# Couplings and inverse products of the two head halves alternate on eight 32x32 tiles of the TensorE array; query turns as transposes

## The chip, the cores and the metric

One core of one Trainium2 chip runs the whole program. The metric is the device time of one execution in microseconds. The kernel before takes 2709.87 us, the median of 3 runs (2707.37 to 2710.03).

## What is computed

Input is x of shape 2 x 4096 x 512 (two sequences, b = 0 and 1). A routing layer, a recurrent attention layer and the routing layer again are applied, each on the layer-normed x and added to it. The attention layer is the part that the change touches, for each of 16 heads of width 32:

```
q, k, v = xWq, xWk, xWv per head; q and k scaled to length 1
alpha = sigmoid(x @ Wa + ba); beta = sigmoid(x @ Wb + bb)
for each row t:                       # state: 32 x 32 for each b and head
    pred  = state . k_t
    state = alpha_t * state + beta_t * (v_t - pred) k_t
    y_t   = state . q_t
out = (rmsnorm(y) * silu(x @ Wg)) @ Wo
```

## The kernel before, in words

The rows of a sequence go through in 32 tiles of 128, each cut into 4 chunks of 32 rows. In a chunk the recurrence is solved in closed form: the couplings of its keys with its keys and queries (a 32 x 64 product for each head and chunk), the inverse of a unit triangular 32 x 32 matrix, the inverse applied to values and keys, and products that carry the result into the output and the state. All of these have 32 x 32 stationary operands, so each uses one of the 16 tiles of the TensorE array: its row quarter is that of the operands' 32 partitions, its column quarter that of the output's 32 partitions. A 32-bit product is two MATMUL records in the trace, each with its weight load; a transpose by TensorE is one.

**Work on TensorE.** `gram` (L913, its matmuls L926) makes the couplings: for each head, chunk c of the keys times chunk c of keys and queries, written to partitions of chunk c. So it uses the four tiles (c, c) of the diagonal. It comes in 4 pieces of 4 heads for each b; heads 0 to 7 lie in one PSUM bank, 8 to 15 in another. `apply_uw` (L931, matmuls L945) applies the inverse, again on the four diagonal tiles. `qe_T` (L950, L961) turns the decayed queries by a plain matmul with the identity, 8 blocks of 128 x 128 in a step. `apply_gy` (L964, matmuls L976 and L983) makes the two sorts of products that need no state; in each of its four rounds r, heads 0 to 7 use tiles (c, c+r) and heads 8 to 15 tiles (c, c+r+2), eight tiles in turn. `chain` (L987, L996) brings the state in, chunk by chunk, on four diagonal tiles; between two of them VectorE turns the new state (`state`, L2556). `dec` (L905) sums decays with a triangular mask. `project` (L845, L847), `proj_g` (L891), `out_proj` (L1011), `hidden` (L1028), `logits` (L1040), `cum` (L899), `ffn` (L836), `slots` (L1048) and the transposes `first_xT`, `last_xT` (L690) are full-size products.

**The way round VectorE and memory.** After `gram`, VectorE multiplies the couplings by masks (`coupling` L2516 into `nn`, `reading` L2524 into `pk`). SyncE's queue stores `nn` of both b in memory and loads them as `blk` with one matrix on each partition (L517, L523). VectorE inverts all 128 matrices there, 30 pairs of small operations (`invert` L2530; L2540, L2542), with other work in between. SyncE stores the result (L531) and loads it back as `E` (L537), and `apply_uw` uses it one step later. GpSimd makes the masks and scaled keys (`beta_mask` L2036, `decay_mask` L2042, `key_written` L2052) and the powers for the norms (`key_power`, `query_power`, L1977).

**Order.** Every engine and SyncE's queue run an order written out by hand: `step_pe` (L1433), `step_dve`, `step_act`, `step_pool`, `step_sp`, one step for each tile, with tiles p, q, r, s of different age in one step, p the newest; `first_...` and `last_...` hold the ends. `free(...)` and `since(...)` are the waits that keep buffers and PSUM banks from being overwritten. `step_pe` before runs, with b behind the tile's letter: uw r0 (4 pieces), va q1, gy r0 round 0, va and k q1, then gy r0 rounds 1 to 3 with gram q0 pieces 0 and 1 between them, q projection q1 (4), chain r0.0, dec q0, chain r0.1, gram q0.2, chain r0.2, dec q1, gram q0.3, logits s1, chain r0.3, gram q1 (4), uw r1 piece 0, cum, out r0.0, uw r1 (3), y_norm r0 and out r0 with query turns r1 between them, gy r1 rounds 0 and 1, slots, gate, gy r1 rounds 2 and 3, gate, ffn, then chain r1.0 to r1.3 with gate products, a transpose of alpha and last_xT between them, and the rest of the full-size work, in it logits r0 and the query turns q0. The last before the next step's uw is the query turn q0.

Of the kernel before, what the change touches and what calls it, by code (L numbers as in the profile page):

```python
# [27 lines left out]
P = 128  # L28
# [7 lines left out]
def build(nc, x, Wq, Wk, Wv, Wa, ba, Wb, bb, Wg, Wo, g_norm, slot_init, slot_scale, w1, b1, w2, b2,  # L36
          wih, whh, bih, bhh, wv, bv, wo, bo, tau, out):
    ctx = ExitStack()
    with ctx:
# [33 lines left out]
        after = sb("after", P)  # L73
        chunk = sb("chunk", P)
# [48 lines left out]
        glx = sb("glx", NC * B * H)  # L123
        vk3 = [vk[b][:, :].rearrange("p (m h e) -> p m h e", m=3, h=H) for b in range(B)]
# [74 lines left out]
        hold_in, e_in = sem2("hold_in"), sem2("e_in")  # L199
        sl_ps, sums1, aT_ps, aT = sem("sl_ps"), sem("sums1"), sem("aT_ps"), sem("aT")  # L200
# [8 lines left out]
        ffn_at = [banks(1, 1), banks(2, 1)]  # L209
        xT_at = [banks(1, 1), banks(7, 1)]  # L210
        k_at = [banks(6, 1), banks(0, 1)]
        q_at = [banks(4, 1), banks(4, 1)]
        va_at = [banks(1, 1), banks(5, 1)]
        vb_at = [banks(5, 1), banks(4, 1)]
        g_at = [banks(0, 1), banks(7, 1)]
        dec_at = [banks(5, 1), banks(0, 1)]
        ones_at = [banks(1, 1)[:, 0:1], banks(6, 1)[:, 0:1]]
        wo_at = [banks(2, 1), banks(0, 1)]
        rxT_at = [banks(1, 1), banks(0, 1)]
        h_at = [banks(3, 1), banks(2, 1)]  # L220
        lg_at = [banks(7, 1)[:, 0:NS], banks(0, 1)[:, 0:NS]]
        y_at = [banks(6, 2), banks(5, 2)]
        cum_at = banks(6, 1)[:, 0:8 * H]
        aT_at = banks(4, 1)[:, 0:P]
        slot_at = banks(2, 1)
        gram_at = [[banks(1, 1), banks(5, 1)], [banks(4, 1), banks(3, 1)]]
        uw_at = [[banks(0, 1), banks(7, 1)], [banks(1, 1), banks(5, 1)]]
        gq_at = [[banks(3, 1), banks(2, 1)], [banks(0, 1), banks(1, 1)]]
# [172 lines left out]
        def _(sp):  # L401
# [112 lines left out]

            def coupling_out(n, b):
                sp.wait_ge(T["nn"][b], 2 * n)
                sp.dma_start(n_dram[b, :, :, :].rearrange("h p t -> p h t"), heads(nn[b])).then_inc(n_out, 16)  # L517
# [9 lines left out]
            def inverse_out(n):  # L527
                sp.wait_ge(inv, n)
                for b in range(B):
                    since(e_in[b], 16 * (n - 1))  # L530
# [59 lines left out]
            def last_sp():  # L590
                store_second(NT - 2, 0)
                hold(NT - 1, 0)
                store_second(NT - 2, 1)
                store_alpha(NT - 3)
                hold(NT - 1, 1)
                inverse_out(NT - 1)
# [2340 lines left out]
```

## Time and profile before

| what | value |
|---|---|
| median of 3 runs | 2709.87 us |
| profiled execution, its own time | 2713.64 us |
| its span, first to last instruction | 2711.0 us |
| PE (matmul) busy | 2597.6 us, 96% |
| DVE (VectorE) busy | 1849.7 us, 68% |
| POOL (GpSimd) busy | 1334.0 us, 49% |
| ACT (ScalarE) busy | 1122.9 us, 41% |

The first 336 us of the span are weights, routing and the set-up; then the 32 tiles of the attention layer are worked off; the last 130 us end the recurrence and run the second routing layer's last part. Busy time of PE is the union of its records, whose ends are modelled; the time that a block costs is the start of the next block less its own start. PEld are weight loads beside the matmuls.

### The profile page before, as it was taken

How to read it: one execution, taken by the hardware profiler on the slowest of the kernel's cores; microseconds unless marked ns; L12 is line 12 of the kernel's file. 1: busy time of each engine (PE TensorE's matmuls, PEld its weight loads, DVE VectorE, ACT ScalarE, POOL GpSimd, SP SyncE). 2: the span in 40 equal slices, each digit the busy share in tenths (PEclk: the TensorE clock that was granted, in tenths of full speed). 3: DMA queues.
4: the chain of work that ended last, by engine and by line, in shares of the span. 5: the costliest groups of instructions: out<-in, count | busy, mean ns of one | idle time of the engine just before them, and what ended most of it. 6: DMA issues, size and time to landing. Idle time of an engine off the chain costs nothing.

```text
span 2711.0 us, 116416 instructions
## 1 busy us (share of the span) xinstructions
PE 2597.6 (96%) x51052; PEld 1857.1 (69%) x51052; DVE 1849.7 (68%) x5306; ACT 1122.9 (41%) x2024; POOL 1334.0 (49%) x1767
## 2 busy tenths in 40 slices
PE   7999879999999999999999999999999999999868
PEld 5788557777766677677766676777667777776643
DVE  6778456776777766676666666666666776777626
ACT  5777324343333333444334444443444334333320
POOL 2222255555555555555555555555555555555510
PEclk9999989999999999999999999999999999999979
DMA  7443022222222222222222222222222222222178
GB/s 232 113 133 115 22 57 66 67 67 67 67 67 61 60 61 63 58 67 67 67 67 67 65 64 66 55 60 62 64 67 67 67 67 67 67 67 58 52 265 326
DMA packets 365963, 224.74 MB, mean 83 GB/s; under 512 B 277584, under 2 KB 294032, under 8 KB 365456
## 3 DMA queue, kind: packets, MB, share of 16 engines
q1 hardware_dynamic: 356240, 200.51, 26.6%
q10 hardware_dynamic: 9216, 16.78, 1.6%
q8 instruction: 402, 6.59, 1.0%
q14 instruction: 105, 0.86, 0.1%
HBM read 125.49 MB, written 74.97 MB: 74 GB/s over the span
## 4 chain that ended last, share of the span: by engine, by line
PE 62%; DVE 15%; issue 10%; ACT 6%; POOL 5%; SPq 1%; DMA 1%; DVEq 0%; ACTq 0%; POOLq 0%
PE psum L847 14%; PE psum L945 5%; PE psum L1011 4%; PE psum L926 4%; PE psum L891 4%; PE psum L976 4%; PE psum L996 4%; PE psum L983 3%; DVE blk L2542 3%; DVE blk L2540 3%; PE psum L753 2%; PE psum L911 2%; PE psum L961 2%; PE psum L1028 2%; POOL sm L1977 2%
## 5 line engine op out<-in xcount | busy, mean ns | idle before, releaser
L847 PE MATMUL psum<-w_all,xnT 128*128 128x512 f32 (+2 forms) x2048 | 751.0, 501 | 6.7 <-DVE pk L2527 6.0
L1977 POOL TENSOR_TENSOR sm<-sm,half 128x1 f32<-128x1 f32 (+1 forms) x384 | 537.0, 1398 | 142.6 <-ACT sm L1672 126.6
L847 PEld LDWEIGHTS psum<-w_all,xnT 128*128 128x128 f32 x2048 | 366.4, 191 | 229.4 <-issue 178.6
L2540 DVE TENSOR_TENSOR blk<-blk 128x30 f32<-128x30 f32 (+14 forms) x960 | 328.0, 342 | 37.1 <-issue 10.6
L2542 DVE TENSOR_TENSOR blk<-blk 128x30 f32<-128x30 f32 (+14 forms) x960 | 324.0, 338 | 33.0
L2009 POOL TENSOR_SCALAR sm<-sm 128x1 f32<-128x1 f32 x64 | 22.4, 351 | 541.1 <-DVE sm L2447 541.1
L891 PEld LDWEIGHTS psum<-xnT,w_all 128*128 128x128 f32 x2048 | 246.7, 191 | 49.1 <-issue 39.9
L891 PE MATMUL psum<-xnT,w_all 128*128 128x128 f32 x2048 | 273.7, 282 | 0.0
L1011 PE MATMUL psum<-w_out,gate 128*128 128x512 f32 x512 | 260.7, 612 | 0.0
L996 PEld LDWEIGHTS psum<-qg,st 32*32 32x32 f32 x8192 | 127.4, 105 | 94.9 <-issue 55.5
L2492 DVE TENSOR_REDUCE sm<-scr 128x16 f32<-128x512 f32 x64 | 43.9, 686 | 201.4 <-ACT scr L1648 201.4
L1695 ACT ACTIVATE qg<-psum 128x256 f32<-128x256 f32 x128 | 42.1, 381 | 322.7 <-PE psum L976 322.7
L996 PE MATMUL psum<-qg,st 32*32 32x64 f32 x8192 | 167.9, 218 | 6.3 <-issue 3.8
L926 PE MATMUL psum<-kqT 32*32 32x64 f32 x8192 | 148.0, 215 | 5.5 <-DVE kqT L2508 2.1
L976 PE MATMUL psum<-pk,uw 32*32 32x64 f32 x8192 | 144.4, 224 | 7.4 <-issue 6.4
L983 PE MATMUL psum<-pk,uw 32*32 32x64 f32 x8192 | 149.6, 225 | 0.7 <-issue 0.7
L926 PEld LDWEIGHTS psum<-kqT 32*32 32x32 f32 x8192 | 124.2, 105 | 38.1 <-issue 26.7
L1028 PEld LDWEIGHTS psum<-rxT,w1T 128*128 128x128 f32 x1024 | 131.1, 194 | 19.9 <-issue 15.3
L945 PEld LDWEIGHTS psum<-vk,E 32*32 32x32 f32 x8192 | 120.8, 105 | 29.1 <-issue 25.2
L1028 PE MATMUL psum<-rxT,w1T 128*128 128x128 f32 x1024 | 140.1, 281 | 0.0
L976 PEld LDWEIGHTS psum<-pk,uw 32*32 32x32 f32 x8192 | 99.9, 103 | 54.4 <-issue 32.8
L945 PE MATMUL psum<-vk,E 32*32 32x64 f32 x8192 | 134.8, 215 | 0.0
(278 smaller groups left out, 4726.4 us busy)
## 6 DMA issues: line engine op xcount, KB each, us to landing
blk<-n_scratch SPq DMA_DIRECT2D x64, 512.0 KB, 4.2
xin<-in_L_attn_x_dram SPq DMA_DIRECT2D x96, 256.0 KB, 3.0
n_scratch<-nn SPq DMA_DIRECT2D x64, 256.0 KB, 4.1
xh<-xc SPq DMA_DIRECT2D x64, 256.0 KB, 2.2
e_scratch<-blk SPq DMA_DIRECT2D x32, 512.0 KB, 2.9
E<-e_scratch SPq DMA_DIRECT2D x64, 256.0 KB, 3.9
x_scratch<-xh SPq DMA_DIRECT2D x62, 256.0 KB, 2.5
rxn<-in_L_attn_x_dram SPq DMA_DIRECT2D x32, 256.0 KB, 3.0
```

Of the source, the lines that this page charges most:

```text
L847: last = mm(dst, xnT[b][:, k * P:(k + 1) * P], w_all[:, k * WK + at:k * WK + at + n], start=(k == 0), stop=(k == KC - 1))
L891: last = mm(g_at[b][:, part * P:(part + 1) * P], w_all[:, at:at + P], xnT[b][:, k * P:(k + 1) * P], start=(k == 0), stop=(k == KC - 1))
L926: last = mm(q32(gram_at[b][part], c, at, 2 * HD), q32(kqT[b], c, h * 2 * HD, HD), q32(kqT[b], c, h * 2 * HD, 2 * HD), start=True, stop=True)
L945: last = mm(q32(uw_at[b][part], c, at, 2 * HD), q32(E[b], c, h * HD, HD), vk3[b][CH * c:CH * (c + 1), n % 2::2 - n % 2, h, :], start=True, ...
L976: last = mm(q32(gq_at[b][hb // 2], hq, (hb % 2 * NC + c) * 2 * HD, 2 * HD), q32(uw[b], c, at + HD, HD), q32(pk[b], c, at, 2 * HD), start=F ...
L983: last = mm(q32(y_at[b], hq, (hb * NC + c) * 2 * HD, 2 * HD), q32(uw[b], c, at, HD), q32(pk[b], c, at, 2 * HD), start=(hb % 2 == 0 and r = ...
L996: last = mm(q32(y_at[b], hq, at, 2 * HD), q32(st[b], hq, x * P + hb * HD, HD), q32(qg[b], hq, at, 2 * HD), start=False, stop=True, skip_gr ...
L1011: last = mm(wo_at[b], gate[b][:, part * P:(part + 1) * P], w_out[:, part * D:(part + 1) * D], start=(part == 0), stop=(part == KC - 1))
L1028: last = mm(h_at[b][:, part * P:(part + 1) * P], w1T[:, k * HID + part * P:k * HID + (part + 1) * P], rxT[b][:, k * P:(k + 1) * P], start= ...
L1977: return g.tensor_tensor(dst, a, half[:, 0:n], ALU.pow)
L2540: own(tt(o, Y[:, 0:rows, s_:s_ + 1].to_broadcast([P, rows, cols]), N[:, s_:s_ + 1, s_ + 1:CH].to_broadcast([P, rows, cols]), ALU.mult))
L2542: ins = tt(Y[:, 0:rows, s_ + 1:CH], Y[:, 0:rows, s_ + 1:CH], o, ALU.add)
```

## The change

In `gram` and `apply_uw` a piece now holds two heads of each half, and the halves alternate. Heads 0 to 7 stay on tiles (c, c); heads 8 to 15 write to the row quarter (c + 2) mod 4 and so use tiles (c, c+2). Couplings and inverse products of heads 8 to 15 thus lie with their halves of 64 partitions exchanged. What multiplies them must lie so too: the inverse of heads 8 to 15 is loaded with halves exchanged back (three DMAs in place of one for each b), the scaled keys of heads 8 to 15 are written aside and copied over by two DMAs for each b, beta by two small ones for each tile, and the decays come from a mask `cross` whose halves are exchanged, made once. `beta_mask` and `key_written` become two operations of half size each; `dec` two products of 256 columns in place of one of 512. `apply_gy` reads the exchanged rows for heads 8 to 15 and writes where it wrote; it still has eight tiles in a round. `qe_T` sets `is_transpose`. All PSUM banks are given out anew, with their `free` waits, and the orders of all engines and of SyncE's queue are new; the loop's steps are cut at another place. `first_pe` gets 55 small products and one transpose (`fill`) before the first real transpose of the layer.

```diff
+            def row_of(c, part):
+                return (c + 2 * part) % NC
             def gram(n, b, piece):
...
+                for k in range(2 * piece, 2 * piece + 2):
+                    for part in range(2):
+                        h = part * H // 2 + k
+                        for c in range(NC):
+                            last = mm(q32(gram_at[b][part], row_of(c, part), k * 2 * HD, 2 * HD), q32(kqT[b], c, h * 2 * HD, HD),
+                                      q32(kqT[b], c, h * 2 * HD, 2 * HD), start=True, stop=True)
+                        if k == H // 2 - 1:
+                            last.then_inc(T["gram_ps"][b], 1)
...
             def apply_uw(n, b, piece):
+                for k in range(2 * piece, 2 * piece + 2):
+                    for part in range(2):
+                        h = part * H // 2 + k
+                        for c in range(NC):
+                            last = mm(q32(uw_at[b][part], row_of(c, part), k * 2 * HD, 2 * HD), q32(E[b], c, h * HD, HD),
...
             def qe_T(n, b, part):
-                       ident[:, :].rearrange("p (c e) -> p c e", c=NC), start=(k == 0), stop=False, skip_group_check=True)
+                       ident[:, :].rearrange("p (c e) -> p c e", c=NC), start=(k == 0), stop=False, is_transpose=True,
...
             def apply_gy(n, b, r):
-                tiles = [(2 * part + k, c, (c + r + 2 * part) % NC) for k in range(2) for part in range(2) for c in range(NC)]
+                tiles = [(2 * part + k, c, (c + r) % NC) for k in range(2) for part in range(2) for c in range(NC)]
...
-                    last = mm(q32(y_at[b], hq, (hb * NC + c) * 2 * HD, 2 * HD), q32(uw[b], c, at, HD),
+                    last = mm(q32(y_at[b], hq, (hb * NC + c) * 2 * HD, 2 * HD), q32(uw[b], row_of(c, hb // 2), at, HD),
...
             def dec(n, b):
-                mm(dec_at[b], after[:, :], dr[b][:, :], start=True, stop=True).then_inc(S["dec_ps"], 1)
+                for part, mask in enumerate((after, cross)):
+                    last = mm(dec_at[b][:, part * D // 2:(part + 1) * D // 2], mask[:, :], dr[b][:, part * D // 2:(part + 1) * D // 2],
...
+            def key_across(n, b):
+                sp.wait_ge(S["kd"], both(n, b))
+                for k in range(2):
+                    sp.dma_start(heads(pk[b], 2)[half_of(k), H // 2:H, HD:2 * HD],
+                                 kdt[b][half_of(1 - k), :].rearrange("p (g t) -> p g t", t=HD)).then_inc(kd_in[b], 16)
+            def beta_across(n):
+                sp.wait_ge(S["be"], n)
...
             def inverse_in(n, b):
-                sp.dma_start(heads(E[b]), e_dram[b, :, :, :].rearrange("h p t -> p h t")).then_inc(e_in[b], 16)
+                out = e_dram[b, :, :, :].rearrange("h p t -> p h t")
+                sp.dma_start(heads(E[b])[:, 0:H // 2, :], out[:, 0:H // 2, :]).then_inc(e_in[b], 16)
+                for k in range(2):
+                    sp.dma_start(heads(E[b])[half_of(k), H // 2:H, :], out[half_of(1 - k), H // 2:H, :]).then_inc(e_in[b], 16)
...
             def key_written(n, b):
-                g.tensor_tensor(heads(pk[b], 2)[:, :, HD:2 * HD], heads(kn[b]), bc(s(b, "bel")), ALU.mult).then_inc(S["kd"], 1)
+                for part, into in enumerate((heads(pk[b], 2)[:, 0:H // 2, HD:2 * HD], kdt[b][:, :].rearrange("p (g t) -> p g t", t=HD))):
+                    last = g.tensor_tensor(into, heads(kn[b])[:, part * H // 2:(part + 1) * H // 2, :],
...
```

`beta_mask` waits for beta's copy (`be_in`), the first `apply_gy` of a tile for the keys' (`kd_in`), `apply_uw` for all three parts of the inverse (`e_in` at 48 n).

The new `step_pe` is in this order: va q1.1, uw r0 (4), k q1.0 and 1, query turns r0 (2), gy r0 rounds 0 to 2, k and q projections q1 in turn (4), gy r0 round 3, q q1 (2), gram q0.0, chain r0.0, gram q0.1, chain r0.1, gram q0.2, chain r0.2, dec q0, chain r0.3, gram q0.3, dec q1, gram q1 (4), logits s1, cum, out r0 (2), uw r1 (4), out r0.2, query turns r1 (2), y_norm r0, out r0.3, gy r1 rounds 0 and 1, slots, gate (2), gy r1 rounds 2 and 3, gate (3), chain r1.0, last_xT r0, chain r1.1, gate, ffn p, gate, chain r1.2, gate, chain r1.3, hidden r0.0, vb q1.0, first_xT p0, hidden r0.1, k p0.0, out r1 with y_norm, transpose of alpha, k p0.1, vb q1.1, va, k and q p0, logits r0, last_xT r1, hidden r1, vb p0, first_xT p1, va p1.0. In SyncE's queue `beta_across` stands ahead of `coupling_out`, `key_across` of b = 0 ahead of the first `hold`, and that of b = 1 behind the last `inverse_in`. On VectorE, `reading` of b = 1 moves to later places of the inversion, `first_sum` of b = 0 stands ahead of `state` r1.1, and `query_sums` of b = 1 ahead of `state` r0.0.

## Rows read from the trace of the kernel before

**Rows 1.** The page, part 1: busy time, share of the span, instructions.

```profile
span 2711.0 us, 116416 instructions
PE 2597.6 (96%) x51052; PEld 1857.1 (69%) x51052; DVE 1849.7 (68%) x5306; ACT 1122.9 (41%) x2024; POOL 1334.0 (49%) x1767
```

**Rows 2.** Busy time in stretches: the steady stretch, the end, one step.

```profile
core 0: us, PE busy (x) PEld busy (x) DVE busy (x) ACT busy (x) POOL busy (x), PEclk, DMA share, GB/s
404.50:2562.00 2157.50, 2140.14 (x46779) 1517.86 (x46778) 1506.04 (x4122) 865.55 (x1518) 1203.39 (x1523) 1.00 0.24 64
2562.00:2711.00 149.00, 104.62 (x1330) 63.55 (x1328) 71.68 (x162) 27.41 (x51) 14.25 (x27) 0.83 0.78 277
...
1298.90:1369.00 70.10, 69.65 (x1528) 49.52 (x1527) 49.28 (x136) 28.46 (x51) 39.52 (x50) 1.00 0.25 65
```

**Rows 3.** Timeline of PE, 1307 to 1311 us: start, us, line, count.

```profile
1307.16 1.99 PE L945 MATMUL psum<-vk,E 32*32 32x64 f32 x128
1309.08 1.24 PE L847 MATMUL psum<-w_all,xnT 128*128 128x288 f32 x4
1310.24 0.45 PE L976 MATMUL psum<-pk,uw 32*32 32x64 f32 x32
1310.51 0.59 PE L983 MATMUL psum<-pk,uw 32*32 32x64 f32 x32
```

**Rows 4.** Timeline of PE, 1323 to 1331 us.

```profile
1324.58 0.65 PE L926 MATMUL psum<-kqT 32*32 32x64 f32 x32
1325.05 0.62 PE L996 MATMUL psum<-qg,st 32*32 32x64 f32 x32
1325.61 1.12 PE L911 MATMUL psum<-dr,after 128*128 128x512 f32 x2
...
1327.51 0.63 PE L1040 MATMUL psum<-w2T,hT 128*128 128x64 f32 x4 [0.20 <-ACT dr L1684]
1328.07 0.65 PE L996 MATMUL psum<-qg,st 32*32 32x64 f32 x32
1328.63 1.99 PE L926 MATMUL psum<-kqT 32*32 32x64 f32 x128
1330.42 0.65 PE L945 MATMUL psum<-vk,E 32*32 32x64 f32 x32
```

**Rows 5.** Timeline of PE, 1338 to 1340 us, the first and last two pieces.

```profile
1338.40 0.45 PE L976 MATMUL psum<-pk,uw 32*32 32x64 f32 x32
...
1339.38 0.49 PE L983 MATMUL psum<-pk,uw 32*32 32x64 f32 x29
1339.81 1.08 PE L1048 MATMUL psum<-rxn,alpha 128*64 128x512 f32 x4
```

**Rows 6.** Timeline of PE, 1300 to 1306 us.

```profile
1300.74 0.63 PE L1040 MATMUL psum<-w2T,hT 128*128 128x64 f32 x4 [0.21 <-ACT gate L1667]
1301.20 1.08 PE L847 MATMUL psum<-w_all,xnT 128*128 128x256 f32 x4
1302.12 0.61 PE L961 MATMUL psum<-ident,qa 128*128 128x128 f32 x4
1302.57 1.06 PE L1028 MATMUL psum<-rxT,w1T 128*128 128x128 f32 x8
1303.46 1.02 PE L847 MATMUL psum<-w_all,xnT 128*128 128x512 f32 x2
1304.32 1.05 PE L1028 MATMUL psum<-rxT,w1T 128*128 128x128 f32 x8
1305.21 0.60 PE L690 MATMUL psum<-ident,xn 128*128 128x128 f32 x4
1305.65 1.14 PE L847 MATMUL psum<-w_all,xnT 128*128 128x288 f32 x4
```

**Rows 7.** Timeline of DVE: a state turn between chains; the inversion's last pair.

```profile
1325.74 0.32 DVE L2559 STREAM_TRANSPOSE st<-psum 128x128 f32<-128x128 f32 x1 [0.23 <-PE psum L996]
...
1369.66 0.21 DVE L2542 TENSOR_TENSOR blk<-blk 128x30 f32<-128x30 f32 x1
```

**Rows 8.** DMA issues: KB each, median us to landing.

```profile
E<-e_scratch SPq DMA_DIRECT2D x64, 256.0 KB, 3.9
```

**Rows 9.** Timeline of SyncE's queue and PE's next step.

```profile
1372.77 1.90 SPq L537 DMA_DIRECT2D E<-e_scratch  x2
...
1377.29 1.99 PE L945 MATMUL psum<-vk,E 32*32 32x64 f32 x128
```

**Rows 10.** Groups on POOL of the step at 1299 us: busy, mean ns.

```profile
L2058 POOL TENSOR_TENSOR pk<-kn,sm 128x512 f32<-128x512 f32 x2 | 2.1, 1047 | 0.2
...
L2009 POOL TENSOR_SCALAR sm<-sm 128x1 f32<-128x1 f32 x2 | 0.7, 358 | 15.8 <-DVE sm L2447 15.8
```

More of the change, by code:

```diff
@@ L123, in build @@
         glx = sb("glx", NC * B * H)
+        gsw = sb("gsw", B * H)
+        kdt = [sb(f"kdt{b}", D // 2) for b in range(B)]
         vk3 = [vk[b][:, :].rearrange("p (m h e) -> p m h e", m=3, h=H) for b in range(B)]
@@ L917, in gram @@
                     pe.wait_ge(S["qt"], both(n, b))
-                    if b == 0:
-                        free((n, (S["va"], both(n, 0))))
-                if piece == 2:
-                    if b == 0:
-                        free((n, (S["draw"], both(n, 0))))
-                for h in range(piece * NC, (piece + 1) * NC):
-                    at = (h - part * H // 2) * 2 * HD
-                    for c in range(NC):
-                        last = mm(q32(gram_at[b][part], c, at, 2 * HD), q32(kqT[b], c, h * 2 * HD, HD),
-                                  q32(kqT[b], c, h * 2 * HD, 2 * HD), start=True, stop=True)
@@ L1148, in last_pe, with fill @@
+            def fill(n, turned):
+                for i in range(n):
+                    c = i % NC
+                    mm(q32(y_at[1], c, i // NC % 8 * 2 * HD, HD), q32(ident, c, c * HD, HD), q32(ident, c, 0, HD), start=True, stop=True)
+                for c in range(turned):
+                    tr(q32(y_at[1], c, 0, HD), q32(ident, c, c * HD, HD), q32(ident, c, c * HD, HD))
+            def last_pe():
+                proj_va(NT, 1, 1)
                 apply_uw(NT - 1, 0, 0)
@@ new lines, in first_pe @@
+                chain(2, 1, 3)
+                hidden(2, 0, 0)
+                proj_vb(3, 1, 0)
+                first_xT(4, 0)
+                hidden(2, 0, 1)
+                proj_k(4, 0, 0)
+                out_proj(2, 1, 0)
+                out_proj(2, 1, 1)
+                y_norm(2, 1)
+                out_proj(2, 1, 2)
+                out_proj(2, 1, 3)
+                alpha_T(1)
+                proj_k(4, 0, 1)
+                proj_vb(3, 1, 1)
+                proj_va(4, 0, 0)
+                proj_k(4, 0, 2)
@@ new lines, in first_pe, with step_pe @@
+                proj_va(4, 0, 1)
+                proj_q(4, 0, 0)
+                proj_k(4, 0, 3)
+                logits(2, 0)
+                last_xT(2, 1)
+                proj_q(4, 0, 1)
+                proj_q(4, 0, 2)
+                hidden(2, 1, 0)
+                proj_q(4, 0, 3)
+                proj_vb(4, 0, 0)
+                hidden(2, 1, 1)
+                first_xT(4, 1)
+                proj_vb(4, 0, 1)
+                proj_va(4, 1, 0)
+            def step_pe(p, q, r, s, u):
+                proj_va(q, 1, 1)
@@ L2265, in set_masks @@
                 own(tt(after[:, :], chunk[:, :], upto[:, :], ALU.subtract))
+                for k in range(2):
+                    own(ts(cross[:, k * P // 2:(k + 1) * P // 2], after[:, (1 - k) * P // 2:(2 - k) * P // 2], 1.0, None, ALU.mult))
                 own(ts(w, pi, 31, None, ALU.bitwise_and))
```

1203 lines of the change are left out of this document (603 added, 600 removed).

## The prediction

> **What bounds the kernel now.** I read four views in this order. The page's busy line [rows 1] shows PE at 2597.6 of 2711.0 us and the next engine at 68%. The stretches [rows 2] show where that holds: from 404.5 to 2562 us PE is busy 2140.14 of 2157.50 us at granted clock 1.00, the full 2.4 GHz, and only the end, 149 us, has real gaps. So the steady part is bound by how fast PE gets through its blocks. One step takes 1377.29 - 1307.16 = 70.13 us between the same block of two tiles [rows 3, 9]; 2157.5 / 70.13 gives 31 steps. In a step DVE has 49.28 us and POOL 39.52 us of work [rows 2], some 20 and 30 us of room. Third, PE's timeline, for the price of each block (the next start less its own). Last, the timelines of DVE and of SyncE's queue, for what could become late when PE is faster.
>
> **Price of a tile product.** Four diagonal tiles: 128 records of the couplings start at 1328.63 and their successor in the same mode at 1330.42 [rows 4]: 1.79 us, 14.0 ns a record. Eight tiles in turn: the first 32 records of a burst take 1310.51 - 1310.24 = 0.27 us [rows 3], 8.4 ns. Two whole rounds of the eight-tile products, 128 records, start at 1338.40 and hand over to full-size work at 1339.81 [rows 5], 1.41 us; the same handover after 128 diagonal records costs 1309.08 - 1307.16 = 1.92 us [rows 3], which is 0.13 us over the 1.79. Less this 0.13 the eight tiles run at 1.28 / 128 = 10.0 ns. So a record moved from four tiles to eight is worth between 4.0 ns (sustained) and 5.6 ns (a burst of 32).
>
> **The change part by part, for one step.**
> - Couplings of b = 0, 128 records, stand as four single pieces of 32 between chains. The bursts of 32 are their nearest row: from 0.47 us (1325.05 - 1324.58, [rows 4]) to 0.27 us each, -0.80 us.
> - Couplings of b = 1 and both inverse products, 384 records in rows of 128, are nearest to the sustained price: 384 x 4.0 ns = -1.54 us; at the burst price it would be -2.15.
> - Query turns: 8 blocks, each two records before and one after. Four records of the plain turn take 1302.57 - 1302.12 = 0.45 us, four of TensorE's own transposes, a record each, 1305.65 - 1305.21 = 0.44 us [rows 6]. The record costs the same and half of 16 go: 8 x 0.11 = -0.90 us.
> - The waits of the two logits products, 0.20 and 0.21 us [rows 4, 6], were on PSUM banks that others still read. Their banks and places are new; I take them as gone, -0.41.
> - Mode changes between 32x32 and full size: 14 stretches of tile products in the old step, 13 in the new. Leaving tile mode costs the 0.13 above. Entering it: four records of 288 columns between tile stretches take 1310.24 - 1309.08 = 1.16 us [rows 3], where 0.92 for four of 256 [rows 6] scales to 1.04, so 0.12. One stretch less is -0.25; bounds 0 and -0.3.
> - Decay sums: four records of 256 columns for two of 512. Four of 256 columns take 1302.12 - 1301.20 = 0.92 us, two of 512 take 1304.32 - 1303.46 = 0.86 [rows 6]: +0.06 twice, +0.12.
> - State chain of b = 0. A chain at 1325.05 is followed by a state turn that begins at 1325.74 and takes 0.32 us [rows 4, 7], so the next chain can start no sooner than 1.01 us after the last. With a piece of couplings between them the cover was 0.56 + 0.47 = 1.03 us, exactly enough; now it is 0.56 + 0.27 = 0.83, so 0.2 us of idle appear twice. The same holds for the second chain of b = 1, which has only one transpose of four records (0.44) ahead of it, and query sums now stand before the first state turn. Bound: 0 (if the handovers hide it) to 1.2 us; I take +0.40.
> - Hidden by PE: POOL's scaled keys and beta masks in halves. A 128x512 operation takes 1047 ns [rows 10]; four are split, and a half costs at least half and at most the whole, so +0 to +4.2 us on an engine that sits idle 15.8 us a step before one group alone [rows 10]. Without that cover the keys would be late for SyncE's new copies.
> - Hidden, but close: the way of the inverse. The last pair of the inversion ends at 1369.87 [rows 7], E's loads are issued at 1372.77 [rows 9], land after 3.9 us [rows 8] at 1376.7, and the product starts at 1377.29: 0.6 us of room. PE's road from the couplings to that product gains the logits s1 (1328.07 - 1327.51 = 0.56) and va p1 (two of about 1.0), and loses the query turns q0 (0.9), half of r1's (0.45) and 0.5 of the inverse product of b = 1: about 0.7 us longer than now, so more room. Three DMAs for one add two issues, at most 1.90 / 2 = 0.95 us each [rows 9], and the couplings of both halves of b = 1 now end together, which puts one more masking operation behind them. I put 0 here and keep 1.9 - 0.6 - 0.7 = 0.6 as the bound for the issues alone.
> - Copies of keys and beta: their nearest row is the 3.9 us of E. The keys of b = 0 are copied half a step ahead, beta is wanted after the decay rows. 0 taken, 1 us kept as bound.
>
> Sum: -0.80 - 1.54 - 0.90 - 0.41 - 0.25 + 0.12 + 0.40 = -3.38 us a step, x 31 = -105 us. The head and the tail wait for other engines and give nothing; `fill` stands in a wait. Against the profiled execution's 2713.64 us: 2609; the median shown lies 3.8 us below that execution, so **2605 us**.
>
> **A rule of the skill that speaks against it.** Rows 3 and 5 show eight tiles at 8.4 to 10.0 ns where four take 14.0, though the eight share four row quarters in pairs. The Trainium skill, TensorE: Matmul & The Clock Gate, "What overlaps and what doesn't", says that a weight load overlaps matmuls in flight only where the row group differs. By that rule the second tile of a row quarter would gain nothing; the trace disagrees as far as the products of keys and writes go, and the rule is left as the first rival.
>
> **Rivals.**
> 1. *The eight tiles don't help here.* Couplings and inverse products keep 14.0 ns: two tiles of one row quarter would stand in each other's way with these operands. Then -0.90 - 0.41 - 0.25 + 0.12 and no state stall, -1.44 x 31 = -45, about 2665. Against it stand rows 3 and 5, with the same two banks alternating. Chance 0.08.
> 2. *Latency takes most of it.* The room of 0.6 us at E, the state chains and the norm's way (query sums, GpSimd's power, scale, turn, couplings) are all near their limit at a period of 70.1; the stalls come to 1.9 us or more instead of 0.4. -3.38 + 1.5 = -1.9 x 31 = -58, about 2650. For it: [rows 4, 7] show two of them without slack. Chance 0.17.
> 3. *Slower.* E's exchanged load has two DMAs of 64 partitions behind the first, and the copies of keys and beta share SyncE's queue, each holding what stands behind it until its source is ready. If E lands more than 0.6 + 3.4 = 4.0 us later than now, beyond the 3.9 us of a whole load [rows 8], the product waits for it every step and the gain is gone; at three loads one after another, +7.8 - 4.0 = +3.8 x 31 = +118, about 2824; at its mildest just over 2710. Chance 0.07.
> 4. *The burst price holds throughout* and stalls stay hidden: -0.80 - 2.15 - 0.90 - 0.41 - 0.25 + 0.12 = -4.39 x 31 = -136, about 2574. Chance 0.18.
>
> The forecast has the rest, 0.50, with 2590 to 2625 as its own range. A measurement here can tell about 0.2%, 5.4 us, from no change. Range over all: from rival 4 to a little over rivals 1 and 2, 2568 to 2668. Faster 0.90, same 0.03, slower 0.07.
>
> **What would show it.** In the profile after: L926 and L945's successors in blocks of 128 records 1.1 to 1.3 us after their start (not 1.8); query turns with two records a call and 256 in all; a step of 66.7 us; DVE busy as before, its share up; idle of PE before chains and before the inverse product under 1 us a step. Wrong would be: 14 ns a record (rival 1); PE's idle in the steady stretch over 2 us a step with DVE's state, POOL's power or E as releaser (rival 2); L945 waiting for the DMA of E or the first L976 for that of the keys (rival 3).

## The result, and where the time went

The changed kernel takes 2665.72 us (median of 4 runs, 2656.03 to 2676.29) where the kernel before takes 2709.95 us (2707.37 to 2717.83): ratio 0.9831, interval 0.9801 to 0.9862. That is 44 us faster: inside the outer range of 2568 to 2668, outside the forecast's own 2590 to 2625, and less than half of the 105 us that the prediction worked out. Times and ratios here are of runs within 1.5% of their kernel's fastest, which leaves out three of e12's seven. The profiled execution of the changed kernel has a span of 2674.5 us and lasted 2676.29 us, the longest of the four.

The page's busy line and queue table, for [rows 1]; q8 is the queue that fetches TensorE's program, with packets, MB and share:

```profile
span 2674.5 us, 117064 instructions
PE 2524.0 (94%) x51035; PEld 1788.1 (67%) x51035; DVE 1821.2 (68%) x5308; ACT 1050.8 (39%) x1962; POOL 1357.9 (51%) x1895
...
q8 instruction: 402, 6.59, 1.0%
```

The 31 steady steps between the inverse products of the first and the last stage, first in the kernel before, then in the changed one. The columns are those of [rows 2]:

```profile
390.50:2576.80 2186.30, 2161.16 (x47286) 1533.61 (x47285) 1521.68 (x4163) 878.60 (x1539) 1219.96 (x1542) 1.00 0.24 64
```

```profile
396.75:2537.13 2140.38, 2072.14 (x47154) 1454.44 (x47153) 1492.86 (x4162) 804.74 (x1476) 1240.87 (x1663) 1.00 0.27 69
2537.13:2674.50 137.37, 103.51 (x1292) 60.98 (x1292) 62.10 (x135) 20.52 (x41) 8.90 (x18) 0.77 0.81 292
```

PE's busy time fell by 2161.16 - 2072.14 = 89.0 us, 2.87 us a step. Its idle time rose from 25.1 to 68.2 us, 1.39 us a step. The steady part is 45.9 us shorter, 69.04 us a step against 70.53; the head is 6.3 and the tail 3.2 us longer. So most of the expected gain in busy time came, and nearly half of it was given back as idle time. The chain of waits of TensorE shows who got it (line waited for, total us, times, longest):

```profile
PE psum L972 <- ACT dr L1743: 24.1, 31, 0.8
...
PE psum L1041 <- DVE st L2629: 13.2, 34, 0.7
PE psum L1021 <- issue: 10.7, 10, 2.4
...
PE psum L988 <- DMA E<-e_scratch: 6.5, 1, 6.5
...
PE psum L1041 <- issue: 4.7, 5, 3.5
PE psum L972 <- issue: 4.5, 7, 2.0
```

The first two come in every step and are semaphore waits. "Issue" is different: in the steady steps TensorE stood for 0.2 to 1.75 us at a time with nothing listed that it waited for (the longer ones are in the tail).

PE's timeline of one undisturbed step; columns as in [rows 3], L972 is now the couplings, L988 the inverse product, L1006 the query turn, L1041 the state chain, L953 the decay sums:

```profile
1364.08 1.47 PE L988 MATMUL psum<-vk,E 32*32 32x64 f32 x128
1365.48 1.98 PE L881 MATMUL psum<-w_all,xnT 128*128 128x512 f32 x4
1367.30 0.60 PE L1006 MATMUL psum<-ident,qa 128*128 128x128 f32 x4
1367.83 0.45 PE L1021 MATMUL psum<-pk,uw 32*32 32x64 f32 x32
...
1376.19 0.45 PE L972 MATMUL psum<-kqT 32*32 32x64 f32 x32
1376.45 0.67 PE L1041 MATMUL psum<-qg,st 32*32 32x64 f32 x29
...
1376.97 0.52 PE L972 MATMUL psum<-kqT 32*32 32x64 f32 x28
1377.89 0.59 PE L1041 MATMUL psum<-qg,st 32*32 32x64 f32 x28 [0.40 <-DVE st L2629]
...
1381.54 0.70 PE L953 MATMUL psum<-dr,after 128*128 128x256 f32 x2
1382.07 0.59 PE L953 MATMUL psum<-dr,cross 128*128 128x256 f32 x2
1383.44 1.47 PE L972 MATMUL psum<-kqT 32*32 32x64 f32 x128 [0.78 <-ACT dr L1743]
1384.84 0.55 PE L1090 MATMUL psum<-w2T,hT 128*128 128x64 f32 x3
```

128 records of the inverse product hand over after 1365.48 - 1364.08 = 1.40 us; the same handover took 1.92 [rows 3]. The couplings of b = 1 take 1384.84 - 1383.44 = 1.40 us for 1.79 [rows 4]. A record of a tile product costs 10 ns, as forecast, once the 0.13 us of the handover to full-size work is taken off. But those couplings write the PSUM bank that ScalarE is still reading for the decay rows of b = 1: the sums end at 1382.7, the reading takes 0.60 us, and TensorE stands for 0.78 us. The state chain waits 0.40 us, because VectorE now does the query sums (1376.93 to 1377.53) before the first state turn.

### The profile page after: what moved, and what is told of

Its sections match the earlier page's. It is cut to its first block, busy times and chain, and to the rows that moved or that the text cites. A ratio compares the mean times of both kernels' runs of the same rounds, so it can differ in the third digit from the quotient of the medians.

```text
span 2674.5 us, 117064 instructions
## 1 busy us (share of the span) xinstructions
PE 2524.0 (94%) x51035; PEld 1788.1 (67%) x51035; DVE 1821.2 (68%) x5308; ACT 1050.8 (39%) x1962; POOL 1357.9 (51%) x1895
## 3 DMA queue, kind: packets, MB, share of 16 engines
q8 instruction: 402, 6.59, 1.0%
## 4 chain that ended last, share of the span: by engine, by line
PE 78%; DVE 8%; issue 5%; POOL 4%; ACT 2%; SPq 1%; DMA 1%; POOLq 0%; DVEq 0%; ACTq 0%
PE psum L881 26%; PE psum L936 8%; PE psum L1060 8%; PE psum L1078 5%; PE psum L1041 4%; PE psum L1021 3%; PE psum L988 3%; PE psum L1028 3%; PE psum L727 3%; PE psum L790 2%; PE psum L972 1%; PE psum L953 1%; PE psum L872 1%; POOL dm L2107 1%; PE psum L1098 1%
## 5 line engine op out<-in xcount | busy, mean ns | idle before, releaser
L881 PE MATMUL psum<-w_all,xnT 128*128 128x512 f32 (+2 forms) x2048 | 740.1, 502 | 1.9 <-ACT xnT L1687 1.4
L936 PEld LDWEIGHTS psum<-xnT,w_all 128*128 128x128 f32 x2048 | 245.0, 194 | 58.1 <-issue 49.2
L936 PE MATMUL psum<-xnT,w_all 128*128 128x128 f32 x2048 | 275.4, 285 | 0.8 <-issue 0.6
L1041 PE MATMUL psum<-qg,st 32*32 32x64 f32 x8192 | 175.1, 220 | 25.9 <-DVE st L2629 13.2
L1041 PEld LDWEIGHTS psum<-qg,st 32*32 32x32 f32 x8192 | 133.6, 106 | 68.2 <-DVE st L2629 39.3
L972 PE MATMUL psum<-kqT 32*32 32x64 f32 x8192 | 124.2, 221 | 32.6 <-ACT dr L1743 24.1
L1028 PE MATMUL psum<-pk,uw 32*32 32x64 f32 x8192 | 149.3, 226 | 0.0
L1021 PE MATMUL psum<-pk,uw 32*32 32x64 f32 x8192 | 136.0, 224 | 11.1 <-issue 10.7
L972 PEld LDWEIGHTS psum<-kqT 32*32 32x32 f32 x8192 | 97.6, 103 | 73.1 <-issue 71.9
L1021 PEld LDWEIGHTS psum<-pk,uw 32*32 32x32 f32 x8192 | 91.9, 104 | 69.1 <-issue 65.1
L2143 POOL TENSOR_TENSOR sq<-sq 128x256 f32<-128x256 f32 x64 | 48.2, 753 | 166.5 <-ACT sq L1767 166.5
L1060 PEld LDWEIGHTS psum<-w_out,gate 128*128 128x128 f32 x512 | 87.7, 192 | 65.8 <-issue 61.5
L2629 DVE STREAM_TRANSPOSE st<-psum 128x128 f32<-128x128 f32 x256 | 78.3, 306 | 73.6 <-PE psum L1041 71.6
```

The lines of the kernel that those rows point to most:

```text
L881: last = mm(dst, xnT[b][:, k * P:(k + 1) * P], w_all[:, k * WK + at:k * WK + at + n], start=(k == 0), stop=(k == KC - 1))
L936: last = mm(g_at[b][:, part * P:(part + 1) * P], w_all[:, at:at + P], xnT[b][:, k * P:(k + 1) * P], start=(k == 0), stop=(k == KC - 1))
L972: last = mm(q32(gram_at[b][part], row_of(c, part), k * 2 * HD, 2 * HD), q32(kqT[b], c, h * 2 * HD, HD), q32(kqT[b], c, h * 2 * HD, 2 * HD) ...
L1021: last = mm(q32(gq_at[b][hb // 2], hq, (hb % 2 * NC + c) * 2 * HD, 2 * HD), q32(uw[b], row_of(c, hb // 2), at + HD, HD), q32(pk[b], row_of ...
L1028: last = mm(q32(y_at[b], hq, (hb * NC + c) * 2 * HD, 2 * HD), q32(uw[b], row_of(c, hb // 2), at, HD), q32(pk[b], row_of(c, hb // 2), at, 2 ...
L1041: last = mm(q32(y_at[b], hq, at, 2 * HD), q32(st[b], hq, x * P + hb * HD, HD), q32(qg[b], hq, at, 2 * HD), start=False, stop=True, skip_gr ...
```

## A count of TensorE's blocks

TensorE's instructions are fetched from memory as the engine goes. Each float32 product is four of them (two weight loads, two matmuls), each with a record in the trace; the waits that stand alone have one too. Numbered in order, a step has 3072 of them in both kernels. The 402 packets of 16 KB on q8 carry 256 instructions each, so a step uses 12 packets, and each block of 256 begins at the same place of every step. Worked out from the traces: a packet takes 1.04 us (median), and two packets never start less than 3.21 us apart. Where TensorE stands at "issue" in the steady steps, the first matmul behind the gap is one whose number leaves the same remainder on division by 256 (196 to 198; which one depends only on where the count starts), and it starts 1.4 us (1.3 to 1.6) after the end of a packet. This holds in all 20 traces of this document: of the 1025 gaps over 0.15 us with no releaser between 400 and 2480 us, every one lies at the start of a block, and every one ends 1.2 to 1.7 us after a packet's end. So these gaps are waits for the program. A block that is all tile products (128 matmul records and their weight loads) takes 1.4 us, and then the next packet must already be there. The table below counts, in 23 steady steps, the idle time over 0.15 us at those numbers.

The spacing of 3.2 us is not what holds TensorE up as a rule. In the changed kernel's 19 of these gaps the packet that ended them had begun 3.5 to 6.7 us after the packet before it, and 1.0 to 3.8 us after TensorE had begun the block before. The packet came late because it began late, and no run shows what it waited for.

The Trainium skill, Runtime: NRT & Kernel Launch, "Instruction fetch mechanics", says that an engine's program arrives in blocks of 16 KiB, 256 instructions, fetched while the current one runs, at a cost that is mostly hidden. The trace agrees on the size (402 packets, 6.59 MB) and, in the kernel before, on the cost. The runs below do not agree on the cost: where the blocks begin at other places of the step it is not hidden, up to 5.87 us a step.

## The experiments

**The changed kernel once more.**

> The changed kernel once more, as the mark for the others. Both theories: 2656 to 2676 us, as in its first four runs; in its trace again 0.78 us of idle before the couplings of b = 1 in every step (decays' bank), and two spots of 0.1 to 0.4 us before state chains.

Measured: 2664.58 us, ratio 0.9827 (0.9813 to 0.984). This is the reference for what follows; its steady step is 68.92 us.

**Plain query turns in the changed kernel, and turns in transpose mode alone.**

```diff
 # e1, changed kernel
-start=(k == 0), stop=False, is_transpose=True,
+start=(k == 0), stop=False,
 # e2, kernel before
-start=(k == 0), stop=False, skip_group_check=True)
+start=(k == 0), stop=False, is_transpose=True, skip_group_check=True)
```

> The changed kernel with the query turns as plain matmuls with the identity again (8 more records a step). Theory A (the turns' saving is real and on PE's path): 0.9 to 1.0 us a step more, +28 to +31 us on the changed kernel. Theory B (what PE saves there it loses in later waits): under +10 us.

> The kernel before with nothing but the query turns as transposes. Theory A: 0.9 us a step less, -28 us, about 2682. Theory B (each saving is eaten by the latency from the inverse to its product, which had 0.6 us of room): -15 us or less, with idle before the inverse product.

Measured: e1 2839.71 us, ratio 1.0485 (1.0462 to 1.0507); e2 2813.27 us, ratio 1.0372 (1.0352 to 1.0391). Each, by itself, is over 100 us slower than the kernel that it was made from, though one adds and the other removes the same work. No expectation held. Two steps of e2, the shortest and the longest of the middle of its run:

```profile
1497.14:1566.73 69.59, 68.93 (x1520) 48.23 (x1520) 49.33 (x136) 28.52 (x51) 39.59 (x51) 1.00 0.24 65
2163.19:2240.41 77.22, 72.67 (x1520) 50.61 (x1519) 47.85 (x136) 28.51 (x51) 39.61 (x51) 0.96 0.22 59
```

The same 1520 matmuls take 69.59 us or 77.22. The short step shows what the turns bring, about 1 us; the long one has 4.6 us of idle, and its mean granted clock is 0.96. A step of e2 has 3056 instructions, of e1 3088: the blocks' places move by 16 a step, and return after 16 steps. In e1 too a good step comes back (69.94 us at 1512.15). This was the first sign that the place of the blocks matters.

**Four tiles instead of eight.**

```diff
-                return (c + 2 * part) % NC
+                return c
```

> The changed kernel with all tile products of the couplings and the inverse back on the four diagonal tiles (halves still alternate, the exchanged rows are read at their old place, so heads 8 to 15 come out wrong; all work, waits and orders stay). Theory A (eight tiles save what the price of a record says, but the window between the last query product and the couplings of b = 1 is set by waits, so what the single coupling pieces save is lost there): +1.5 to +1.9 us a step, +45 to +58 us. Theory B (eight tiles save the full 2.3 to 2.8 us a step and the new order costs elsewhere): +72 to +87 us. Theory C (eight tiles are worth little with these operands): under +25 us.

This kernel leaves out the exchange of the rows of heads 8 to 15 in the products while the rest still exchanges them, so the values of these heads are wrong; the instructions are the same ones. Measured: 2737.36 us, ratio 1.0092 (1.0079 to 1.0106), 72.8 us over the changed kernel, 2.35 us a step. That looked like the 2.34 of the prediction, and it is not the same sum: `row_of` also serves the two output products, which stood on eight tiles already in the kernel before. By line (from the start of each matmul to the next, idle over 0.05 us left out, us a step):

```
              before    e9      e3   changed (e0)
couplings      3.67    3.66    4.22    3.51
inverse pr.    3.97    3.98    3.84    2.81
output pr.     5.91    5.97    7.25    5.86
state chain    4.71    4.71    4.30    4.34
query turns    1.96    1.07    0.97    0.97
gate proj.     7.96    8.09    8.16    8.18
out proj.      7.24    7.24    7.43    7.43
idle           0.48    0.73    0.99    1.75
whole step    70.61   70.05   71.25   69.05
```

Of e3's loss 7.25 - 5.86 = 1.39 us a step is the output products'. What is new on eight tiles gains 4.22 - 3.51 = 0.71 on the couplings and 1.03 on the inverse products against e3. The table also prices the new order by itself: on the same four tiles the couplings rose from 3.67 to 4.22. Of this, 0.13 is that b = 1 now hands over to full-size work (1.92 us for 1.79); the rest was not taken apart. Rival 1 is out all the same: the tiles do help, on the inverse products by 1.16 us a step against before.

**The order without the new waits.** In the short form below, g is a coupling piece of b = 0, c a state chain of b = 0, d0 and d1 the decay sums of the two b, G the couplings of b = 1, L the logits; where the expectations of e11, e14 and e16 name the couplings or sums of heads 8 to 15, those of b = 1 are meant (and of b = 0 where e14 has heads 0 to 7); on VectorE qs is the query sums, s a state turn, ks and kt the key scale and turn, qq and qt those of the query.

```diff
 # e4
-g0 c0 g1 c1 g2 c2 d0 c3 g3 d1 G L       VectorE: qs s0 s1 s2 ks kt qq qt s3
+g0 c0 d0 c1 d1 c2 g1 g2 c3 g3 L G       VectorE: qs s0 ks s1 kt s2 qq qt s3
 # e5
+g0 c0 g1 c1 g2 c2 d0 c3 d1 L g3 G
 # e6, VectorE alone
+s0 qs s1 s2 ks kt qq qt s3
```

> The changed kernel with the window before the couplings of b = 1 in another order. PE: coupling piece 0, chain 0, decay sums b = 0, chain 1, decay sums b = 1, chain 2, coupling pieces 1 and 2, chain 3, piece 3, logits, couplings of b = 1. VectorE: query sums, state 0, key scale, state 1, key turn, state 2, query scale, query turn, state 3. Theory A (that window lost 1.9 us a step to the decays' bank and to state chains with too little beside them): the waits go and logits lie in what is left of them, -1.2 to -1.6 us a step, -37 to -50 us on the changed kernel, about 2617 to 2630. Theory B (the norm's way through GpSimd's power ends last anyway): under -0.4 us a step, -12 us.

> The changed kernel with only the order behind the decay sums of b = 1 changed: logits and the last coupling piece of b = 0 go between them and the couplings of b = 1. Theory A: the 0.78 us wait on the decays' bank is filled, -0.6 to -0.8 us a step, -18 to -25 us. Theory B (the query turn is late next, right behind): -0.2 us a step at most beyond what the logits fill, under -8 us.

> The changed kernel with the first state turn of b = 0 ahead of the query sums of b = 1 on VectorE, nothing else. Theory A: chain 1 starts 0.3 us sooner, and the query turn ends 0.3 us later but still before the decays' bank is free: -0.3 us a step, -9 us. Theory B (the query turn's way sets the window): no change or up to +9 us.

Measured: e4 2722.47 us, ratio 1.003 (1.0015 to 1.0046); e5 2718.14, 0.9999 (0.9977 to 1.0021), its runs 2689 to 2735; e6 2695.4, 0.9935 (0.9914 to 0.9956). All three are slower than the changed kernel. TensorE's waits in e4:

```profile
PE psum L972 <- issue: 47.2, 32, 2.0
...
PE psum L1021 <- issue: 14.1, 14, 2.4
PE psum L1041 <- issue: 9.1, 19, 2.6
```

Both semaphore waits are gone, as meant. At the same couplings TensorE now stands for 47.2 us with nothing listed, in place of 24.1 for the bank and 4.5 with nothing listed. In all of the 23 steps counted, this gap lies at number 708 of the step. In the changed kernel the 0.78 us wait lies in the block just before that place, where it gives the next packet time to arrive. In e6 the wait of the first state chain is gone as well, so the query sums were its cause; but the 0.78 us stayed, another bank wait grew from 0.7 us in all to 13.9, and the idle time with nothing listed rose from 0.35 (e0) to 0.79 us a step:

```profile
PE psum L944 <- ACT sq L1767: 13.9, 22, 1.5
```

**The key copy cut to an eighth.**

```diff
-sp.dma_start(heads(pk[b], 2)[half_of(k), H // 2:H, HD:2 * HD],
+sp.dma_start(heads(pk[b], 2)[half_of(k), H // 2:H // 2 + 1, HD:2 * HD],
```

> The changed kernel with the copies of the keys cut to one head of eight (keys of heads 9 to 15 are then wrong). Theory D (the copy's small packets slow the fetch of PE's instructions while tile products use them up fastest, which makes the idle of 0.4 to 1.8 us about 34 us into some steps): those gaps go, -10 to -20 us. Theory A (the gaps are rare and are there without the copy): under -6 us.

It leaves the keys of heads 9 to 15 uncopied. Measured: 2668.57 us, ratio 0.9834 (0.982 to 0.9848), against 2664.58 for e0. The copy's traffic is not what holds TensorE.

**The blocks moved, the steps untouched.** `fill` stands once, ahead of the first step, and its products are used by nobody. Each of them is four instructions.

```diff
 # e8                    # e10, e11 (e4's order)   # e12         # e13         # e16
-fill(55, 1)             -fill(55, 1)              -fill(55, 1)  -fill(55, 1)  -fill(55, 1)
+                        +fill(87, 1)              +fill(51, 1)  +fill(47, 1)  +fill(59, 1)
```

> The changed kernel without the 55 small matmuls and the turn that precede the first step (222 instructions of TensorE's program). The steady steps are untouched; only the place at which the 256-instruction blocks of the program begin within a step moves, by 34 instructions, against the changed kernel. Theory F (TensorE's program arrives in 16 KB blocks, 12 a step, no closer than some 3.3 us apart, and where a block begins decides whether a wait for it shows): the time moves though no step has changed, by anything between -20 and +100 us, and the idle time put down to nothing (issue) moves with it. Theory W (only the waits for banks and states and the records' prices count): 2664 less at most 1 us, 2661 to 2667.

> The changed kernel with 87 instead of 55 small matmuls ahead of the first step: the blocks of the program begin half a block (128 instructions) elsewhere in each step, and the kernel has 32 x 4 more instructions once, under 2 us. Theory F: the time moves by over 10 us, up or down. Theory W: 2664 to 2667.

> The changed kernel with 51 instead of 55 small matmuls ahead of the first step: 16 instructions fewer, so that each block of the program begins 16 instructions later in the step. In the changed kernel's trace the stalls of TensorE that no semaphore explains all lie at the instruction whose number leaves 196 to 198 on division by 256, 0.4 us a step at the 1476th; 34 instructions earlier (e8) cost 38 us. Theory F: a plateau, 2650 to 2675 us, with the leftover stalls at other records of the step. Theory W: 2664.

> As e12, with 47 small matmuls: the blocks begin 32 instructions later. Theory F: still between 2645 and 2680 us, no jump before some 50 instructions, since only then a block falls wholly into couplings and inverse products. Theory W: 2664.

> The changed kernel with 59 small matmuls ahead of the first step: each block of the program begins 16 instructions earlier in the step, the side on which 34 instructions cost 38 us, where the side of e12 cost 68 us for 16. Theory F: 2655 to 2690 us; under 2664 only if the 0.2 us a step at the couplings of heads 8-15 (the 709th instruction) go and those at the 1476th do not grow, which in e8 had grown to 1.3 us. Theory W: 2664.

```
        shift of the blocks    time, us          ratio to before           idle at block numbers,
        within a step                            (interval)                us a step (before: 0.04)
e13     32 later               2846.98           1.0504 (1.0483-1.0526)    3.25
e12     16 later               2723.88           1.0031 (0.9997-1.0066)    2.16
e0      0                      2664.58           0.9827 (0.9813-0.9840)    0.43
e16     16 earlier             2680.66           0.9873 (0.9857-0.9890)    0.65
e8      34 earlier             2703.23           0.9974 (0.9964-0.9984)    1.33
e10     128 earlier            2891.93           1.0657 (1.0639-1.0675)    5.87
```

Not one instruction of a step differs in these kernels, and they span 227 us. e12's seven runs spread from 2702 to 2762 us, and its idle time is that of the longest, so it stands high beside the 2724. Of e10's 227 us over e0 the listed idle time makes (5.87 - 0.43) x 31 = 169; with the last record's time ahead of each gap it is 198, and the mean granted clock is 0.966 for 0.98. Waits of e10:

```profile
PE psum L1028 <- issue: 76.1, 54, 2.4
PE psum L1021 <- issue: 42.1, 31, 4.3
PE psum L972 <- issue: 30.7, 31, 1.5
PE psum L946 <- issue: 29.1, 30, 1.4
PE psum L972 <- ACT dr L1743: 24.2, 31, 0.8
```

The semaphore wait is the same 24 us as in the changed kernel; all that is new has no releaser. One of these gaps in e10's timeline of PE, and e10's queues from 1466 to 1471 us, with a single packet of program:

```profile
1467.84 0.23 PE L1028 MATMUL psum<-pk,uw 32*32 32x64 f32 x2
1470.21 0.44 PE L1028 MATMUL psum<-pk,uw 32*32 32x64 f32 x27 [2.14 <-issue]
```

```profile
q8 instruction: 1, 0.02, 1.5%
q1 hardware_dynamic: 70, 0.01, 1.0%
```

TensorE stops in the middle of a run of like products, with all operands long there. The packet started at 1467.60, took 1.18 us, and TensorE went on 1.43 us after its end. In e8 the gap falls on the gate projection (31 times at L936, 40.1 us), 34 instructions ahead of a block start that costs the changed kernel next to nothing (L936, 0.6 us in all): full-size work is not free of these waits.

The plateau expected for e12 and e13 did not come. It rested on packets that are always there 3.3 us after the one before; then nothing should have been lost for some 50 instructions. The chip lost 59 us at 16. In e12 the gap at number 709 is either absent (11 of 23 steps) or up to 2.5 us long. In a step of e13 a packet started 5.64 us after the one before, though TensorE had entered the block before it 3.3 us earlier. So it is shown that TensorE waits for packets, and where; when the next one is asked for is not settled, and the loss at a given place can't be worked out in advance from these runs.

**Turns with the blocks held still.** To e2, 16 empty instructions a step were added, which brings a step back to 3072.

```diff
+                       is_transpose=True,
...
+                    pe.nop().then_inc(padded, 1)
+                    pe.nop().then_inc(padded, 1)
```

> The kernel before with the query turns in transpose mode and nothing else of the change, and in place of the 16 instructions that a step saves so, 16 empty instructions behind the turns, so that a step has 3072 instructions again and the blocks of the program begin where they did. Theory F: the cost of the turns alone in transpose mode (2813 us) came from the drifting blocks; with the blocks still the turns bring their 0.9 to 1.0 us a step: 2710 - 30 = 2680 us, 2675 to 2692. Theory W, or a transpose mode that is slow in itself: about 2810 us again.

Measured: 2693.68 us, ratio 0.9931 (0.9919 to 0.9943): 119.6 us less than e2, with more instructions. (e1 had no such run; all its 85 gaps with no releaser lie at block starts, as do the 78 of e2.) The turns are worth 17.1 us instead of the 28 forecast. Their own line fell as forecast, from 1.96 to 1.07 us a step; 0.25 came back as idle and 0.13 at the gate projection. The logits' waits are what they were (10.1 us in 31 waits for the gate, in both kernels). New in the steady steps is a wait of the product `slots` (L1052) for VectorE, where the kernel before had none over 0.15 us; the rest is at block starts, 3.5 us for 1.5:

```profile
PE psum L1052 <- DVE xh L2574: 5.2, 29, 0.5
```

**The two new orders with other blocks.** e11 is e4 with 87 products ahead; e14 and e17 are e5 with 51 and 59, e15 is e6 with 51.

```diff
-fill(55, 1)
+fill(87, 1)     # e11; fill(51, 1) in e14 and e15, fill(59, 1) in e17
```

> The window's new order of e4, with the blocks of the program half a block elsewhere. Theory F: the 47 us that TensorE stood at the couplings of heads 8-15 with nothing listed go or change, the time leaves 2722 by over 15 us, at best to 2630. Theory W (the new order itself is bad): 2722 again, within 5.

> The order of e5 (the decay sums of heads 0-7 and 8-15 and the logits as cover of the bank wait) with 51 small matmuls. Theory F: e5's stalls of 0.95 us a step at the 708th instruction go in part, 2718 falls by over 15 us, at best to 2640. Theory W (the order itself is bad): 2718 within 5.

> The order of e6 (the first state scaling ahead of the query sums on VectorE) with 51 small matmuls. Theory F: 2695 changes by over 8 us, at best to 2645. Theory W: 2695 within 5.

> The order of e5 with 59 small matmuls. In e14 the stall at the 708th instruction had grown from 0.95 to 1.5 us a step with 16 instructions fewer, so with 16 more it should shrink. Theory F: 2718 falls by over 20 us, to 2645 to 2700. Theory W (the order is bad in itself): 2718 within 5.

Measured: e11 2872.04 us, ratio 1.059 (1.0575 to 1.0605); e14 2740.73, 1.011 (1.0096 to 1.0124); e15 2767.19, 1.021 (1.0188 to 1.0232); e17 2704.03, 0.9953 (0.9931 to 0.9974). The orders depend on the blocks' place as the changed kernel does: 16 instructions either way move e5 by +23 and -14 us (e14 had been expected to fall). "Bad in itself by a fixed amount" is out; that the orders also open waits of their own is not (e17 has 20.3 us of the wait at L944 that e6 has). But none of the tried places makes them better than the changed kernel, and e17 fell by less than the 20 us I had asked for. No version was found that is faster than the changed kernel.

## Why the prediction was right in sign and too large

The step that failed is the sum: it priced every block of PE by the record and let idle time change by nothing (-0.41 for the logits waits, +0.40 for the state chains). Measured, a step's busy time fell by 2.87 us where the sum had 3.37, and its idle time rose by 1.39 where the sum had 0.

- *Inverse products.* With the couplings of b = 1 they were 384 records at 4.0 ns. The inverse products' 256 fell from 3.97 to 2.81 us, 1.16 for the 1.02 forecast. Right. The b = 1 couplings fell by 0.39 for 0.51, since full-size work stands behind them now.
- *Single coupling pieces, -0.80.* Mis-sized, by its place rather than its price. A piece of 32 between other work does take 0.26 us (1376.45 - 1376.19). But two of the four are followed by a chain that waits. From 1376.97 to 1377.89 the same 0.26 us piece holds TensorE for 0.92: 0.40 of idle and the last product's 0.24 us, which is no longer covered by a successor. All couplings fell from 3.67 to 3.51 us where -1.31 was forecast: the tiles gave 0.71 and the order took 0.55 back (e3). The chains gave 0.37 that was not forecast.
- *Query turns, -0.90.* Their line fell by 0.99 in the changed kernel and 0.89 in e9. Right as a price; alone they bring 0.55 a step.
- *Logits waits, -0.41.* They went. But "their banks and places are new; I take them as gone" looked only at the waits that left. The couplings of b = 1 now share a bank with the decay sums just ahead, 0.78 us in each of 31 steps. This term was missing.
- *State chains, +0.40.* The bound of 1.2 held. The first waits 0.40 us and the second about 0.1; from chain to chain it is 1.44 us (1377.89 - 1376.45) and 1.09, where it was 1.03. That is +0.47 us, and DVE's query sums ahead of the turn, which the prediction named, are the reason.
- *Blocks of the program.* Not in the prediction at all. Idle at block numbers rose from 0.04 to 0.42 us a step; with what hides under the last record, the gaps between two starts sum to 0.08 before and 0.73 after. That is up to 20 us of the missing 61. Whether the forecast step of 66.7 us could be had with the program as it arrives is not shown.
- *Projections.* Gate and out projections became 0.2 us longer each, which no term foresaw. It is not the clock: the out projection takes 7.24 us in each of 23 steps before and 7.43 in each of 23 after, and e3, whose steady steps have next to no such gaps, has the same 7.43 and 8.16. What changed for them is their neighbours: the gate projection, for one, now hands over to a state chain three times a step instead of twice. Only in the two steps with a stretch at the half clock does the gate projection take over 9 us.
- *Decay sums, +0.12, and mode changes, -0.25.* The sums measured +0.01. The mode changes were not priced by a run of their own. The product `ffn` (L872), which hands over to the gate projection where it had handed over to a chain, fell from 1.48 to 1.06 us, which no term foresaw either.
- *Head and tail, "give nothing".* They cost 9.4 us more in the profiled execution. `fill` adds 222 instructions there. In e0 the first step starts at 389.27 us, so the head's part is within what runs differ by.
- *Rivals.* Rival 2 (about 2650, latency takes most) was 16 us low, and right on the state chains; the norm's way, POOL and E were not late. Rival 1 gives 2665, the very number measured, for a reason that is false: the records cost 10 ns, not 14. The rule of the Trainium skill, TensorE: Matmul & The Clock Gate, "What overlaps and what doesn't", behind that rival does not describe these products: two tiles of one row quarter run at 10 ns a record here. Rival 3: L988 waited for E once, 6.5 us at the last tile; its 0.6 us of room was enough. Its 2824 should have been 2828 by its own sum (2709.87 + 118). Rival 4 had the burst price; sustained it is 10 ns.
- *What would show it.* The prediction had written: idle in the steady stretch over 2 us a step with those releasers means rival 2. It is 68.2 / 31 = 2.20 us. The largest releaser, the bank with 0.78 us a step, was not on the list, nor was the program with 0.38; DVE's state, with 0.35, was.

That the measured time lies in the outer range is owed to the upper end that rivals 1 and 2 had set, not to the sum. The parts do not add: e4 took the 0.78 us wait away, and the wait for the next packet took its place. What is shown is that idle time at the waits and idle time at the blocks replace one another. What the changed kernel would take if its program were always there was not tried, for no kernel here has that.

## What to carry to other kernels

When an engine's stream is dense in tiny instructions, its program is a transfer that can come late: count the instructions per stretch, and set them against the packets on the instruction queue before a per-record gain is summed up. Gaps with no releaser that always come at the same instruction number, counted modulo the instructions of a packet, are its mark. Where a kernel stands at such a limit, an edit that changes the number of instructions per step, or ahead of the loop, can cost more than it is worth for this reason alone; hold the count still (as e9 does) when one part is to be priced. And when products move to another PSUM bank, ask who reads that bank last, for the old waits that go say nothing about the new ones.

## What the runs showed of the hardware

- Two packets of TensorE's program (16 KB, 256 instructions) start no less than 3.2 us apart in any of the 20 traces. At a gap with no releaser the engine goes on 1.2 to 1.7 us after a packet's end (median 1.4, 1025 gaps).
- After a gap the granted clock can drop to 0.50, that is 1.2 of 2.4 GHz. Two stretches of the changed kernel, the gap and what follows, and the whole step around them:

```profile
1325.80:1327.50 1.70, 0.00 (x0) 0.00 (x0) 1.46 (x8) 0.00 (x0) 0.00 (x0) 1.00 0.11 25
1327.90:1331.20 3.30, 3.30 (x92) 3.13 (x83) 2.97 (x10) 0.66 (x2) 0.00 (x0) 0.50 0.26 86
1291.88:1364.08 72.20, 68.95 (x1525) 48.46 (x1524) 47.90 (x135) 26.16 (x49) 40.30 (x55) 0.98 0.26 67
```

This step took 72.20 us where the undisturbed one beside it, from 1364.08 to 1432.37, took 68.29. Set side by side at the same instructions, it was 0.6 us behind before the gap, 2.6 behind it, and 4.0 at the end of the stretch at the half clock: a gap of 1.75 us cost 3.4, about twice itself. Over the steady steps the granted clock is 0.96 in e13, where the same products also show 2159.99 us of busy time instead of 2072.14:

```profile
392.99:2711.90 2318.91, 2159.99 (x47154) 1500.67 (x47153) 1496.63 (x4162) 805.62 (x1476) 1242.09 (x1663) 0.96 0.25 64
```

- A transpose-mode product of 128 columns costs the same 0.11 us a record as a plain matmul (four in 0.44 and 0.45 us, [rows 6]) and needs half the records.
